# Self-attention of a decoder layer: how four heads get their causal mask and their row maxima

## The reference, cut to what matters

```
q = einsum(xh, Wq) * scale;  k = einsum(xh, Wk) * scale;  v = einsum(xh, Wv)     # 16 heads of 32
scores = einsum('bihc,bjhc->bhij', q, k)
scores = where(j > i, -inf, scores)
attn = softmax(scores)
y = einsum('bhij,bjhc->bihc', attn, v) @ Wu.T + bu
x = layernorm(x + y)
```

## Time and profile before

| | us |
|---|---|
| median of 3 runs | 1410.64 |
| the profiled execution | 1409.47 |
| its span in the trace | 1407.5 |
| PE busy | 1381.1 (98%) |
| DVE busy | 922.0 (66%) |
| ACT busy | 733.0 (52%) |
| POOL busy | 570.2 (41%) |

### The profile page before, as it was taken

The page is one execution under the profiler, slowest core; times in us unless marked ns, Lnnn a source line. Parts: engine busy times, 40 slices in busy tenths (PEclk is TensorE's granted clock), DMA queues, the critical chain, the costliest instruction groups (busy, mean ns, idle before and its releaser), DMA issues.

```text
span 1407.5 us, 28532 instructions
## 1 busy us (share of the span) xinstructions
PE 1381.1 (98%) x10017; PEld 1208.2 (86%) x10017; DVE 922.0 (66%) x1911; ACT 733.0 (52%) x1989; POOL 570.2 (41%) x475
## 2 busy tenths in 40 slices
PE   7999999999999999999999999999999999999997
PEld 3677777777899999999999988999999999999775
DVE  4589999999667667765777673345443454536687
ACT  4588888888565666566655554222222222322232
POOL 2567767776575656656565620000000000010264
PEclk9999999999999999999999999999999999999999
DMA  7114322336386877676769553011010100000353
GB/s 213 39 43 107 105 81 76 104 105 172 100 230 192 223 201 214 172 230 195 218 178 266 157 156 100 0 27 26 0 27 0 26 13 20 30 1 31 105 186 122
DMA packets 133463, 157.94 MB, mean 112 GB/s; under 512 B 62688, under 2 KB 70880, under 8 KB 133392
## 3 DMA queue, kind: packets, MB, share of 16 engines
q1 hardware_dynamic: 133392, 157.01, 39.7%
HBM read 105.61 MB, written 35.78 MB: 100 GB/s over the span
## 4 chain that ended last, share of the span: by engine, by line
PE 65%; issue 3%; POOL 2%; DVE 2%; ACT 0%; DMA 0%; POOLq 0%; DVEq 0%; ACTq 0%
PE banks L1528 16%; PE banks L1557 11%; PE banks L1023 9%; PE banks L1007 9%; PE banks L1036 6%; PE banks L1559 6%; PE banks L992 5%; PE banks L977 1%; POOL o_r L2103 1%; PE banks L1989 1%; PE banks L1053 1%; POOL o_rstd L2111 1%; DVE s_dot L1222 1%; PE banks L2020 0%; DMA x_scratch<-a_xn 0%
## 5 line engine op out<-in xcount | busy, mean ns | idle before, releaser
L461 ACT ACTIVATE s_p<-banks,a_nmax 112x224 f32<-112x224 f32 (+1 forms) x512 | 198.5, 413 | 58.3 <-DVE a_nmax L572 58.2
L759 POOL TENSOR_TENSOR s_p<-s_p,a_rinv 112x896 f32<-112x896 f32 (+1 forms) x128 | 164.7, 1308 | 116.7 <-DVE a_rinv L580 113.6
L1502 POOL CAST m_hi<-w_raw 128x2048 fp32r<-128x2048 f32 x1 | 2.3, 2267 | 407.8 <-PE banks L1528 407.8
L1645 ACT ACTIVATE f_gate<-f_gate 128x448 f32<-128x448 f32 x90 | 52.2, 580 | 198.5 <-DVE f_gate L1768 198.5
L1765 DVE TENSOR_TENSOR f_gate<-banks,f_xg_early 128x448 f32<-128x448 f32 x45 | 28.1, 624 | 189.6 <-PE banks L1559 189.6
L1369 POOL TENSOR_TENSOR x_cx_lo<-s_cx_raw,x_cx_hi 125x512 fp32r<-125x512 f32 x96 | 121.3, 1301 | 31.1 <-ACT x_cx_hi L1136 31.0
L571 DVE TENSOR_REDUCE a_nmax<-banks 112x1 f32<-112x224 f32 x256 | 97.8, 382 | 23.2 <-PE banks L277 22.4
L461 ACT ACTIVATION_READ_ACCUMULATOR s_p<-banks,a_nmax 112x1 f32 x512 | 111.7, 218 | 0.0
L294 PEld LDWEIGHTS banks<-identity,s_p 112*112 112x112 f32 x768 | 87.7, 134 | 21.6 <-issue 2.1
L294 PE MATMUL banks<-identity,s_p 112*112 112x112 f32 x768 | 105.0, 260 | 1.2 <-POOL s_p L759 0.7
L1362 POOL TENSOR_TENSOR s_ct<-s_ct_raw,s_ct 128x750 fp32r<-128x750 f32 x60 | 98.5, 1676 | 0.2 <-ACT s_ct L1111 0.2
(11 more groups left out here) (255 smaller groups left out, 3720.4 us busy)
## 6 DMA issues: line engine op xcount, KB each, us to landing
s_ct_raw<-in_ct SPq DMA_DIRECT2D x16, 1500.0 KB, 6.7
s_cx_raw<-in_cx SPq DMA_DIRECT2D x16, 1344.0 KB
a_xt<-in_xt SPq DMA_DIRECT2D x16, 448.0 KB, 6.2
a_xrow<-in_x SPq DMA_DIRECT2D x16, 448.0 KB, 5.7
a_xres<-in_x SPq DMA_DIRECT2D x16, 448.0 KB, 6.4
x_scratch<-a_xn SPq DMA_DIRECT2D x16, 448.0 KB, 3.3
x_scratch<-x_xn SPq DMA_DIRECT2D x16, 448.0 KB, 4.6
x_halves<-x_halves SPq DMA_DIRECT2D x16, 448.0 KB, 3.1
```

The costliest lines, as they stand in the source:

```text
L461: e = act.activation((p1 if c else p0)[:, g, h, :], src, ACT.Exp, bias=nmax[:, g % 2, c, h:h + 1], accum_out=rsum[:, g % 2, c, h:h + 1])
L759: pool.tensor_tensor(p[:, g, :, :], p[:, g, :, :], inv, ALU.mult).then_inc(norm_done, 1)
```

## The change

Heads 0 and 1 keep their mask matmul. Their maxima are taken in two instructions instead of four: one over both second halves, one over both first halves.

Heads 2 and 3 get no mask matmul. DVE adds the mask, negates, writes the result to `p1` or `p0` in SBUF, and gives the negated maximum, all in one instruction for each half. ACT takes the Exp of these heads from SBUF, with scale -1. The banks of heads 2 and 3 are so free when DVE has read them. PE's first score matmul waits for the maxima of the step before, no longer for its Exp.

`norm` goes from DVE to POOL, except for the last batch, whose `norm` stays on DVE. On POOL it stands behind `normalise`. A tile `mask_rows` is added, written once on POOL at the start.

```diff
             def s(n, m, odd, g):
-                last = G - 1
-                for h in range(last):
+                for h in range(MASKED):
                     wait(pe, exp_done, G * (n - 1) + h + 1)
                     pe.matmul(ps_s[0:R, h, R:T + R], identity_b[:], mask[:, :, :], start=True, stop=False, skip_group_check=True)
-                wait(pe, exp_done, G * n)
+                wait(pe, max_done, G * n)
...
-                pe.matmul(ps_s[0:R, last, R:T + R], identity_b[:], mask[:, :, :], start=False, stop=True,
-                          skip_group_check=True).then_inc(s_done, 1)
...
             def exp(n, g, heads):
+                        p = (p1 if c else p0)[:, g, h, :]
+                        scores = ps_s[0:R, h, 0:T] if c else ps_s[0:R, h, T:T + R]
+                        src, sign = (scores, 1.0) if h < MASKED else (p, -1.0)
+                        e = act.activation(p, src, ACT.Exp, scale=sign, bias=nmax[:, g % 2, c, h:h + 1],
...
-            def smax(n, g, heads):
-                for h in heads:
-                    wait(dve, s_done, G * n + h + 1)
-                    dve.tensor_reduce(nmax[:, g % 2, 1, h:h + 1], ps_s[0:R, h, 0:T], AX.X, ALU.max, negate=True)
-                    dve.tensor_reduce(nmax[:, g % 2, 0, h:h + 1], ps_s[0:R, h, T:T + R], AX.X, ALU.max, negate=True)\
+            def smax(n, g):
+                wait(dve, t_done, 3 * (n - 3))
+                wait(dve, s_done, G * (n + 1))
+                dve.tensor_reduce(nmax[:, g % 2, 1, 0:MASKED], ps_s[0:R, 0:MASKED, 0:T], AX.X, ALU.max, negate=True)
+                dve.tensor_reduce(nmax[:, g % 2, 0, 0:MASKED], ps_s[0:R, 0:MASKED, T:T + R], AX.X, ALU.max, negate=True)\
+                   .then_inc(max_done, MASKED)
+
+            def masked_max(n, g):
+                for h in range(MASKED, G):
+                    dve.tensor_tensor_reduce(out=p1[:, g, h, :], in0=ps_s[0:R, h, 0:T], in1=mask_rows[:, :, :].rearrange("p a t -> p (a t)"),
+                                             scale=-1.0, scalar=MOST, op0=ALU.add, op1=ALU.min, accum_out=nmax[:, g % 2, 1, h:h + 1])
+                    dve.tensor_tensor_reduce(out=p0[:, g, h, :], in0=ps_s[0:R, h, T:T + R], in1=mask_rows[:, 1, :],
+                                             scale=-1.0, scalar=MOST, op0=ALU.add, op1=ALU.min, accum_out=nmax[:, g % 2, 0, h:h + 1])\
                        .then_inc(max_done, 1)
...
             def steps(i, odd):                                       # DVE
-                    smax(n, g, (0, 1))
+                    smax(n, g)
                     pt_copy(n - 2, (g - 2) % NG, 1)
-                    smax(n, g, (2, 3))
+                    masked_max(n, g)
...
-                    if g % 2 == 0:
-                        norm(b - 3, g // 2)
...
             def steps(i, odd):                                       # POOL
-                        normalise(n - 1, (g - 1) % NG)
+                        normalise(n - 1, (g - 1) % NG, rows_stored=b - 3 if g % 2 == 0 else None)
...
+                    if g % 2 == 0:
+                        norm(b - 3, g // 2)
                     if g == 3:
                         power(b - 2)
                     if isinstance(n, int) and n == STEPS + 3:
                         first_context_low()
```

More of the change, by code:

```diff
@@ L97, in self_attention @@
         bk = sb("bk", [128, KC, 1])
+        mask_rows = sb("mask_rows", [R, 2, R])
         const_ready = sem("const_ready")
@@ L403, in tensor @@
             z(0, 0, 0, 1)
[L404 removed]
+            pe.wait_ge(const_ready, 10)
             def steps(i, odd):
@@ L723, in gpsimd @@
             pool.memset(mhalf[:], -0.5).then_inc(const_ready, 1)
-            pool.wait_ge(const_ready, 5)
+            pool.memset(mask_rows[:], 0.0).then_inc(const_ready, 1)
+            pool.wait_ge(const_ready, 6)
             pool.affine_select(out=identity[:], in_=identity[:], compare_op=ALU.is_equal, fill=0.0, base=0,
-                               pattern=[[-1, 128]], channel_multiplier=1).then_inc(prep_id, 1)
+                               pattern=[[-1, 128]], channel_multiplier=1).then_inc(const_ready, 1)
             pool.affine_select(out=mask[:], in_=mask[:], compare_op=ALU.is_ge, fill=NEG, base=0,
-                               pattern=[[0, 2], [-1, R]], channel_multiplier=1).then_inc(prep_id, 1)
-            pool.wait_ge(prep_id, 2)
+                               pattern=[[0, 2], [-1, R]], channel_multiplier=1).then_inc(const_ready, 1)
+            pool.affine_select(out=mask_rows[:, 1, :], in_=mask_rows[:, 1, :], compare_op=ALU.is_ge, fill=NEG, base=0,
+                               pattern=[[-1, R]], channel_multiplier=1).then_inc(const_ready, 1)
+            pool.wait_ge(const_ready, 9)
             pool.tensor_copy(identity_b[:], identity[0:R, 0:R]).then_inc(const_ready, 1)
             pool.memset(ones[:], 1.0).then_inc(const_ready, 1)
-            pool.wait_ge(const_ready, 7)
+            pool.wait_ge(const_ready, 11)
             def early(n):
@@ L748, in query_parts, with normalise @@
                 pool.tensor_tensor(z_lo[:], xt[:, odd, 2 * j:2 * j + 2, :], z_hi[:], ALU.subtract).then_inc(parts_done, 1)
-            def normalise(n, g, m=None, odd=None, landed=None):
+            def normalise(n, g, m=None, odd=None, landed=None, rows_stored=None):
                 if not within(n, STEPS):
@@ L757, in normalise, with norm @@
                         wait(pool, xt_in[odd], 16 * landed)
+                    if c == 0 and rows_stored is not None and within(rows_stored, B):
+                        wait(pool, stored, 16 * rows_stored)
                     inv = rinv[:, g % 2, c, :].rearrange("p (h a) -> p h a", a=1).to_broadcast((R, G, w))
                     pool.tensor_tensor(p[:, g, :, :], p[:, g, :, :], inv, ALU.mult).then_inc(norm_done, 1)
+            def norm(b, c):
+                if not within(b, B):
+                    return
+                if isinstance(b, int) and b > 0:
+                    pool.wait_ge(stored, 16 * b)
+                pool.tensor_scalar(xn[:, c, :], r[:, c, :], mv[:, c, 0:1], rstd[:, c, :], ALU.subtract, ALU.mult).then_inc(xn_done, 1)
             def power(b):
```

16 lines of the change are left out of this document (7 added, 9 removed).

## The result

| | before | after |
|---|---|---|
| median, us | 1410.66 (runs beside the changed kernel) | 1443.64 (4 runs, 1442.34 to 1446.2) |
| ratio | | 1.0233, 95% interval 1.022 to 1.0247 |
| span of the profiled execution | 1407.5 | 1441.7 |

A forecast was written before the change was run, and what follows sets the result against it. PE set the period by a hair; the change makes the wait for `opened` on ACT the bound. 1409.5 + 13 (loop) + 4.9 (end) = 1427.4 us, median 1428; range 1405 to 1442.

The forecast's parts named there:

- PE's own saving: Two masks fewer on PE save 0.2 us per step, bounds 0.1 to 0.3; pairs could take 9.72 us.
- The ring: Scores, maxima, Exp, L480, projection, next even scores: grows from 10.09 to 10.50 us per pair and sets the period.
- the first Exp: In the ring: starts later by 0.34 us for wider maxima plus 0.1 for waiting on all four heads.
- The Exp from SBUF: ACT's four Exp of heads 2 and 3 per step cost 24 ns more each, 0.1 us in all.
- The signal from ACT to PE: From the end of L480 to PE's waiting L323: 0.14 us.
- the old ring: Wait chain through `opened` before the change: 10.09 us against PE's 10.12, so 0.03 us of slack per pair.
- DVE at g = 3: Maxima behind g = 3 start 0.17 us later every second pair, 0.35 counted back; up to 0.5 if L617 stays slow.
- `norm` on POOL "costs nothing in the loop": `norm` takes 1.0 us on POOL behind `normalise` and delays nothing in the loop; at 1.3 it would still fit.
- The cover: In the loop `normalise` ends 3.7 us after the scores; DVE's `residual` is due at 4.1, ACT needs it at 5.7.
- The end: End of the stage: `norm` of batch 14 behind L796 delays PE's L323 and cross-attention by 4.9 us, bounds 4.5 to 5.2.
- Faster: Rival: PE still sets the period, -13 us in the loop and +4.9 at the end, 1402 to 1403; chance 14%.
- only the end costs: Rival: the later start is hidden and the stage keeps its time within 3 us; 1415, 1412 to 1419; chance 15%.
- `masked_max` blocked by POOL: Rival: DVE's `masked_max` waits for gaps in POOL's work, 2.5 us per pair, 70 us, near 1495; chance 7%.

The follow-up runs named there:

- single_and_later: e1 with maxima of heads 0 and 1 taken head by head, and PE's first projection matmul behind four transposes: 1401.54 us, ratio 0.9935.
- e1: The changed kernel with `norm` back on DVE, everything else kept: 1420.59 us, ratio 1.0078.
- the two edits that undo it: Each on e1: maxima of heads 0 and 1 head by head, 1409.64 us; PE's first projection matmul behind four transposes, 1415.02 us.
- last_norms_on_dve: The changed kernel with `norm` of batches 13 to 15 on DVE, the others on POOL: 1436.06 us, ratio 1.0178.
- pool_one_scalar: The changed kernel with POOL's `norm` only multiplying by rstd, the subtraction of the mean left out: 1431.35 us, ratio 1.0146.

## Why the prediction was wrong in size

**PE's own saving.** Right in kind, a little high. 9.72 us per pair were forecast without waits; single_and_later shows 9.76 and 9.91, so 0.29 are saved per pair instead of 0.40, within the bounds. PE's weight load for L302 still waits for ACT's L492 there, 7.5 us in 20 times; whether that is the rest isn't shown.

**The ring takes over as the bound.** Right, shown by e1 and by the two edits that undo it. Term by term in e1: the first Exp starts 283.19 - 281.25 = 1.94 us after the scores, where it was 304.60 - 303.13 = 1.47; +0.47 against a forecast of 0.34 + 0.1. The Exp from SBUF were taken as 24 ns longer each, from copies. Over some 50 steps, start to start, those of heads 2 and 3 took 425 and 329 ns from PSUM and take 466 and 372 from SBUF, 42 ns more, 0.17 per step (their scale of -1 is new too). The Trainium skill, "VectorE: DVE Perf Modes", section "The TRN2 errata — SBUF-src ops pay a fixed extra latency per instruction", with its 52 cycles (43 ns), was right here and my value from the copies too low. (The sum that the prediction made of it was too small: 0.07 us more in 28 pairs are 2 us, not 1.)

The signal from ACT to PE took 0.05 us in three of four pairs of the loop; it took 0.14, as the earlier trace rows had it, only in every fourth pair, in the first and last batches, and in the steps without scores. If it took 0.05 before the change as well, the old ring was 10.00 us and had 0.12 of slack, not 0.03. These misses cancel: 10.52 and 10.54 against 10.50. That they cancel so closely was luck; the mechanism was as forecast.

**DVE at g = 3.** Wrong, small. I had 0.17 per second pair, and 0.35 back from a faster L617. In e1 both kinds of pair are alike and the maxima start 0.98 us after the scores behind every g (282.23 - 281.25), so there was no such cost; L617 (now L627) was no faster, 0.54 us at the median. The two heads of `masked_max` take 1.0 us (1.5 forecast), in slots of 0.31 and 0.19 us for 224 and 112 columns, where I had 0.43 and 0.32 from L662; the fixed 0.2 of L662 is not there.

```profile
294.23 0.37 DVE L579 CUSTOM_DVE_ANT_0 s_p<-banks,a_mask_rows 112x224 f32<-112x224 f32 x1
...
294.54 0.26 DVE L581 CUSTOM_DVE_ANT_0 s_p<-banks,a_mask_rows 112x112 f32<-112x112 f32 x1
...
294.73 0.38 DVE L579 CUSTOM_DVE_ANT_0 s_p<-banks,a_mask_rows 112x224 f32<-112x224 f32 x1
```

With the masks and maxima alone the stage was to cost 13 us; e1 costs 10 by the medians, and in the profiles 11.9 from step 8 to step 63 (290.25 against 348.67 - 70.30 = 278.37).

**`norm` on POOL "costs nothing in the loop".** This is the step that failed. It was sized at 1.0 us with bounds of 0.61 and 1.30, from a cast and a sum of two inputs, and takes 2.08, outside of both. The cover was also read at one place only. The prediction took `normalise` to begin 0.17 us after the scores, from the step with g = 2 in the earlier trace rows. At g = 0 it stood behind `power` already before:

```profile
314.28 2.58 POOL L759 TENSOR_TENSOR s_p<-s_p,a_rinv 112x896 f32<-112x896 f32 x2 [0.23 <-POOL a_rstd L766]
```

That is 1.03 us after the scores at 313.25, and 1.51 after them now. At g = 2 the air of the forecast just held: `norm` ends 5.1 us after the scores and L478 does not wait. At g = 0 it ends 6.1 after them, and L319 comes 7.65 after the scores (299.47 - 291.82) instead of 6.46 in e1 (287.71 - 281.25). That is 1.19 us; between two such pairs lies one that loses about 0.95. Over the loop `norm` costs 12.6 us where the prediction had nothing: 302.87 from step 8 to step 63 (374.07 - 71.20) against 290.25 in e1. With 1.0 us, `norm` would have ended at 296.88 there, residual at 297.7, just before ACT was free at 297.78: an estimate from these rows, which fits the 1.2 us that the loop loses with 1.57. So the wrong length was decisive, and the overlooked place was where it hit.

**The end.** The mechanism was as forecast (L780 behind L819, then L611, L478, L319), the size 9.8 instead of 4.9; 8.4 of it are `norm`'s (last_norms_on_dve), and the other 1.4 stand in e1 too. L319 starts 407.22 - 374.07 = 33.15 us after step 63, where 29.7 was forecast (378.4 - 348.67). Of the 3.4, 1.1 are again the length of `norm`. The other 2.3 are that L819 begins 23.03 us after step 63 instead of 20.58 (and takes 0.2 less). In e1 it begins at 22.01: 1.4 of the delay belong to the masks and maxima, as the projection in step 63 waits for L478 there too, 1.5 us. The remaining 1.0 are `norm`: already in the steps ahead PE waits for its chain, 2.04 us at 387.15, where the prediction counted a gain of 0.1. The last 1.4 come after the wait: from L319 to the first cross-attention scores it takes 4.95 us, 3.56 before. The busy times by stretch across PE's idle time (the third number from the end is the granted clock):

```profile
401.00:407.00 6.00, 0.40 (x4) 0.21 (x2) 1.22 (x2) 0.53 (x1) 6.00 (x4) 0.69 0.00 0
407.00:409.00 2.00, 1.78 (x4) 1.36 (x5) 0.68 (x3) 1.45 (x5) 0.72 (x1) 0.50 0.21 60
```

After 5.8 us without work PE came back at half its clock, 1.2 instead of 2.4 GHz, and four L319 took 2.02 us where they took 1.09. The prediction named the idle time and forgot this. With the shorter `norm` of pool_one_scalar the slow stretch cost 2.4 us in its place (5.97 against 3.56).

**The rivals.** "Faster" and "only the end costs" fall with e1. "`masked_max` blocked by POOL" falls too: its 224-column half took 372 to 388 ns in all 128 cases, POOL busy or not.

```profile
L579 DVE CUSTOM_DVE_ANT_0 s_p<-banks,a_mask_rows x128: 372/380/388, 12.9 to 378.4; 112x224 f32<-112x224 f32 x128
```

The sum by the profiles, 34.2 us of span: 11.9 for the ring in the loop (13 forecast), 12.6 for `norm` in the loop (0 forecast), 8.8 behind step 63 (4.9 forecast; 1067.6 us from there to the end, 1058.8 before and 1058.9 in e1), and 0.9 ahead of step 8, less than what differs there from one profile to the next.

## What to carry to other kernels

When an operation goes to another engine, its length there has to come from a row of that same form on that engine; without one, the bound has to be where the cover breaks, not the nearest other instruction. Read the cover in each phase of a loop, not in the phase that happens to be on view. An idle gap of PE costs more than its own length when the clock falls in it. And when work is taken off a full engine, look first at which wait stands a tenth of a us behind it: here the first Exp had to stay early, and the wait for ACT had to move one job back, before the masks taken off PE paid (0.65% faster, with `norm` left on DVE).

## What the runs showed of the hardware

- GpSimd takes 2.08 us for a two-operation tensor_scalar over 112x512 with numbers per row, 1.93 with constants, 1.57 with one operation. DVE takes 0.54 for the same `norm`.
- Two costs on one ring of waits don't add: 32 and 10 us alone, 33 together.
- L627, two numbers wide on DVE, takes 0.84 us at the median and 0.17 at best (0.54 at the median in e1 and 0.55 before). I had counted on it getting faster. POOL's `power` waits for it, so at g = 0 it adds some 0.3 us to the late `norm`. The cause is an instruction on POOL, the subtraction in the query parts, and the rows show it:

```profile
L627 DVE TENSOR_SCALAR a_veps<-a_mv x16: 168/838/900, 92.2 to 414.1; 112x2 f32<-112x2 f32 x16
```

```profile
290.89 1.14 POOL L759 TENSOR_TENSOR s_z_in<-a_xt,s_z_in 128x448 fp32r<-128x448 f32 x1
291.22 0.83 DVE L627 TENSOR_SCALAR a_veps<-a_mv 112x2 f32<-112x2 f32 x1
```

POOL's instruction ends at 292.03, L627 at 292.05. In all profiles of this case, each of the 148 that took more than 0.2 us ended 0.02 or 0.03 us behind this instruction of POOL, and none was long when POOL was idle. L627 has one input, in SBUF; `masked_max`, with one input in PSUM and one in SBUF, never stretched.
